# First attention group's score pieces interleaved with the last six QKV tiles

## What is computed

```python
x = x + 0.5 * ffn(layernorm(x), w1, mean_w1, w2, mean_w2, w3, mean_w3)
x = x + attn(layernorm(x), w_qkv, b_qkv, w_dense, b_dense)
x = x + 0.5 * ffn(layernorm(x), ...)
# attn:
qkv = hidden @ w_qkv.T + b_qkv           # per kv head: 4 q heads, 1 k, 1 v, of 16 columns each
q, k = rope(q, cos, sin), rope(k, cos, sin)
scores = q @ k.T * (1 / 16); scores = where(causal mask, scores, min)
ctx = softmax(scores) @ v                # 32 query heads, 8 kv heads
out = ctx @ w_dense.T + b_dense
```

## Time and profile before

| | |
|---|---|
| runs (3) | 1590.87, 1591.80, 1592.49 us; median 1591.8 |
| the profiled execution | 1592.39 us, of which the trace's span is 1590.7 us |
| PE busy | 1474.8 us, 93% of the span |
| DVE busy | 873.8 us, 55% |
| ACT busy | 643.4 us, 40% |
| QKV tiles 0 to 15 | 530 to 617 us from the span's start |
| stage 0, stage 1 | 626 to 654 us, 654 to 682 us |
| stages 2 to 15 | 682 to 1040 us |

### The profile page before, as it was taken

One profiled execution on the slowest core, in us unless ns is written; L12 is line 12 of the kernel. 1 busy time (PEld: TensorE's weight loads), 2 busy tenths in 40 slices (PEclk: granted clock), 3 DMA queues, 4 the chain that ended last, 5 costly groups with the idle time before them and its releaser, 6 DMA issues.

```text
span 1590.7 us, 25041 instructions
## 1 busy us (share of the span) xinstructions
PE 1474.8 (93%) x9584; PEld 659.8 (41%) x9584; DVE 873.8 (55%) x1375; ACT 643.4 (40%) x903; POOL 149.9 (9%) x217
## 2 busy tenths in 40 slices
PE   0788999899999987799999999989999999999998
PEld 0233444344444443334343444324444444444443
DVE  7979432432544476899999999923431422412212
ACT  4464111121122254388888888781211112112111
POOL 0320000000000143012121212210000000000000
PEclk9989999999999998599999999999999999999999
DMA  9501800000000001000000000024000000000000
GB/s 389 195 0 53 354 0 0 1 0 0 1 0 1 1 1 34 1 2 2 2 2 3 2 3 2 2 102 177 0 0 0 28 0 0 27 0 1 27 0 27
DMA packets 16459, 57.38 MB, mean 36 GB/s; under 512 B 4848, under 2 KB 4848, under 8 KB 15856
## 3 DMA queue, kind: packets, MB, share of 16 engines
q1 hardware_dynamic: 16368, 56.11, 9.1%
HBM read 40.63 MB, written 15.20 MB: 35 GB/s over the span
## 4 chain that ended last, share of the span: by engine, by line
PE 83%; DVE 9%; ACT 3%; issue 3%; DMA 0%; POOL 0%; DVEq 0%; ACTq 0%; POOLq 0%
PE ps L1232 32%; PE ps L1253 16%; PE ps L1491 9%; PE ps L1406 7%; PE ps L1472 5%; PE ps L1393 3%; PE ps L1589 3%; PE ps L1279 2%; PE ps L1226 1%; DVE rowmax L1120 1%; PE ps L1501 1%; DVE wbase L877 1%; ACT probs L706 1%; PE ps L1365 1%; DVE w_raw L842 1%
## 5 line engine op out<-in xcount | busy, mean ns | idle before, releaser
L1232 PE MATMUL ps<-xt_hi,w_all 128*128 128x512 f16 x896 | 283.3, 388 | 42.3 <-DVE w_all L883 19.7
L706 ACT ACTIVATE probs<-ps 128x1024 f32<-128x1024 f32 (+3 forms) x384 | 294.1, 814 | 48.5 <-PE ps L1472 45.5
L1120 DVE TENSOR_REDUCE rowmax<-ps 128x2 f32<-128x1024 f32 (+3 forms) x208 | 237.1, 1140 | 15.7 <-PE ps L1414 7.4
L971 DVE SCALAR_TENSOR_TENSOR hb<-ps,scal,silub 128x512 f32<-128x512 f32 x56 | 42.0, 751 | 266.6 <-PE ps L1232 266.6
L1406 PE MATMUL ps<-ka,qa 48*128 48x512 f16 (+3 forms) x768 | 165.7, 345 | 15.4 <-DVE rowmax L1120 9.2
L1232 PE MATMUL ps<-xt_lo,w_all 128*128 128x512 f16 x448 | 173.9, 388 | 0.0
L1491 PE MATMUL ps<-probs,vs 128*32 128x512 f32 (+3 forms) x1536 | 164.4, 500 | 1.4 <-ACT ctx_sb L725 0.8
L1232 PEld LDWEIGHTS ps<-xt_hi,w_all 128*128 128x128 f16 (+1 forms) x896 | 89.4, 100 | 155.9 <-issue 46.0
L1124 DVE TENSOR_REDUCE rowmax<-ps 128x1 f32<-128x512 f32 x192 | 131.2, 684 | 16.3 <-PE ps L1406 13.5
L1472 PE MATMUL ps<-qa,ka 50*128 50x512 f16 (+3 forms) x768 | 133.3, 330 | 3.7 <-ACT probs L706 3.0
L1253 PE MATMUL ps<-w32b_all,hhib 128*128 (+1 forms) x448 | 133.3, 379 | 0.0
(11 more groups left out here) (154 smaller groups left out, 2160.8 us busy)
## 6 DMA issues: line engine op xcount, KB each, us to landing
spill<-w_all SPq DMA_DIRECT2D x1, 10752.0 KB, 28.8
w32b_all<-spill SPq DMA_DIRECT2D x1, 7168.0 KB, 20.9
x<-x_in SPq DMA_DIRECT2D x4, 1024.0 KB, 5.3
y_out<-x SPq DMA_DIRECT2D x4, 1024.0 KB, 4.2
wbase<-m1t SPq DMA_DIRECT2D x4, 896.0 KB, 12.7
w_raw<-w1t SPq DMA_DIRECT2D x4, 896.0 KB, 14.2
wbase<-m3t SPq DMA_DIRECT2D x4, 896.0 KB, 24.3
w_raw<-w3t SPq DMA_DIRECT2D x4, 896.0 KB, 24.3
```

The source lines that it names most:

```text
L706: nc.scalar.activation(probs[u % PBUF][:, 2 * pair:2 * pair + 2, 0:q1 - q0], wide(("scores", g, (u, pair)))[:, :, 0:q1 - q0], ACT.Exp, sca ...
L971: nc.vector.scalar_tensor_tensor(out=bufs["h"][u][:, :], in0=ps[:, UP, :], scalar=scal[:, 1:2], in1=bufs["silu"][u][:, :], op0=ALU.mult, o ...
L1120: nc.vector.tensor_reduce(dst, src, AX.X, ALU.max).then_inc(pair_taken, 1)
L1232: last = mm(ps[:, bank, :], w[a][:, k, bass.ts(t, P)], xt[b][:, k, :], start=(k == 0 and n == 0), stop=(k == HB - 1 and n == 2))
```

## The change

The three transposes and copies of group 0 now stand after tile 9 (`EARLY = 10` tiles come first). From tile 10 on, each tile's two halves on PE are followed by two of group 0's pieces each, four to a tile; piece 24 comes after tile 15. DVE's reductions are set between the steps of the tile chain in the same way. The transposes of group 1, which stood among the pieces of stage 0, come after tiles 13, 14 and 15. The banks of tiles 10 to 15 are no longer chosen by the parity of i but are turns in `WIDE`, and their `take_raw` counts up `wide_taken` instead of `raw_ready`. Stage 0 of the pipeline loop is gone, and the loop runs from k = 1. What is computed is the same.

```diff
+EARLY = 10
+FIRST_TURNS = [("qk", 0, 0), ("qk", 0, 1), ("qk", 0, 2), ("qkv", 0, 10), ("qkv", 0, 11), ("qkv", 0, 12), ("qkv", 0, 13),
+               ("qk", 1, 0), ("qkv", 0, 14), ("qk", 1, 1), ("qkv", 0, 15), ("qk", 1, 2)]
...
-WIDE = turns(WIDE_TURNS, [("qk", 0, o) for o in range(3)])
+WIDE = turns(WIDE_TURNS, FIRST_TURNS)
...
+    def raw_taken(eng, i):
+
+        if i < EARLY:
+            eng.wait_ge(raw_ready, i + 1)
+        else:
+            eng.wait_ge(wide_taken, drained(("qkv", 0, i)))
...
@@ ACT
-        for i in range(TOKEN_TILES):
+        for i in range(EARLY):
...
-        high_parts(TOKEN_TILES - 1)
         for o in range(3):
             take_qk(0, o)
+        for i in range(EARLY, TOKEN_TILES):
+            take_raw(i)
+            take_v(i)
+            high_parts(i - 1)
+            if i >= TOKEN_TILES - 3:
+                take_qk(1, i - TOKEN_TILES + 3)
+        high_parts(TOKEN_TILES - 1)
...
@@ DVE
-        for k in range(GROUPS + 2):
+        for i in range(EARLY, TOKEN_TILES):
+            r = 4 * (i - EARLY)
+            reduce_piece(0, r)
+            add_turned(i - 1)
+            reduce_piece(0, r + 1)
+            low_parts(i - 1)
+            reduce_piece(0, r + 2)
+            along(i)
+            reduce_piece(0, r + 3)
+        add_turned(TOKEN_TILES - 1)
+        reduce_piece(0, NP_ - 1)
+        split_rowmax(0)
+        low_parts(TOKEN_TILES - 1)
+        for k in range(1, GROUPS + 2):
...
@@ PE
-        pe.wait_ge(raw_ready, TOKEN_TILES)
+        pe.wait_ge(raw_ready, EARLY)
         for o in range(3):
             transpose_qk(0, o)
-        for k in range(GROUPS + 2):
+        for i in range(EARLY, TOKEN_TILES):
+            r = 4 * (i - EARLY)
+            qkv(i, 0)
+            score_piece(0, r)
+            score_piece(0, r + 1)
+            qkv(i, 1)
+            score_piece(0, r + 2)
+            score_piece(0, r + 3)
+            if i >= TOKEN_TILES - 3:
+                transpose_qk(1, i - TOKEN_TILES + 3)
+        score_piece(0, NP_ - 1)
+        for k in range(1, GROUPS + 2):
```

More of the change, by code:

```diff
@@ L103 @@
 ]
+EARLY = 10
+FIRST_TURNS = [("qk", 0, 0), ("qk", 0, 1), ("qk", 0, 2), ("qkv", 0, 10), ("qkv", 0, 11), ("qkv", 0, 12), ("qkv", 0, 13),
+               ("qk", 1, 0), ("qkv", 0, 14), ("qk", 1, 1), ("qkv", 0, 15), ("qk", 1, 2)]
 def turns(period, first):
     out = list(first)
-    for k in range(GROUPS + 2):
-        out += [(what, k - lag, n) for what, lag, n in period if 0 <= k - lag < GROUPS and (what, k - lag) != ("qk", 0)]
+    for k in range(1 if first else 0, GROUPS + 2):
+        out += [(what, k - lag, n) for what, lag, n in period if 0 <= k - lag < GROUPS]
     return {use: n for n, use in enumerate(out)}
 TURN = turns(SINGLE_TURNS, [])
-WIDE = turns(WIDE_TURNS, [("qk", 0, o) for o in range(3)])
+WIDE = turns(WIDE_TURNS, FIRST_TURNS)
 def unit_cols(u):
@@ L677, in take_raw, with take_v @@
                 act.wait_ge(turned_ready, 2 * (i - 1))
-            b0 = 2 * (i % 2)
-            nc.scalar.activation(qkv_raw[i % 2][:, :].rearrange("p (s n) -> p s n", s=2), ps[:, b0:b0 + 2, 0:QKV // 2],
-                                 ACT.Copy, scale=scal[:, 3:4]).then_inc(raw_ready, 1)
+            nc.scalar.activation(qkv_raw[i % 2][:, :].rearrange("p (s n) -> p s n", s=2), qkv_banks(i)[:, :, 0:QKV // 2],
+                                 ACT.Copy, scale=scal[:, 3:4]).then_inc(raw_ready if i < EARLY else wide_taken, 1)
+        def take_v(i):
+            raw_taken(act, i)
+            nc.scalar.copy(v_all[:, i, :, :].rearrange("p h d -> p (h d)"), qkv_raw[i % 2][:, ROT:QKV])\
+                .then_inc(v_ready, 1)
         act.wait_ge(spilled, 16)
-        for i in range(TOKEN_TILES):
+        for i in range(EARLY):
             if i in (6, 7):
@@ L687, in _ @@
             take_raw(i)
-            act.wait_ge(raw_ready, i + 1)
-            nc.scalar.copy(v_all[:, i, :, :].rearrange("p h d -> p (h d)"), qkv_raw[i % 2][:, ROT:QKV])\
-                .then_inc(v_ready, 1)
+            take_v(i)
             if i:
                 high_parts(i - 1)
-        high_parts(TOKEN_TILES - 1)
         for o in range(3):
             take_qk(0, o)
+        for i in range(EARLY, TOKEN_TILES):
+            take_raw(i)
+            take_v(i)
+            high_parts(i - 1)
+            if i >= TOKEN_TILES - 3:
+                take_qk(1, i - TOKEN_TILES + 3)
+        high_parts(TOKEN_TILES - 1)
         def exps(g, u, pair):
@@ L1062, in along @@
         def along(i):
-            dve.wait_ge(raw_ready, i + 1)
+            raw_taken(dve, i)
             if i >= 2:
@@ L1084, in low_parts @@
                                     in1=parts_k[:, i, :, 0:HEAD], op=ALU.subtract).then_inc(qklo_ready, 1)
-        for i in range(TOKEN_TILES + 1):
+        for i in range(EARLY):
             if i in (6, 7):
@@ L1370, in transpose_qk, with qkv @@
             last.then_inc(qkt_full, 1)
-        def qkv(i):
+        def qkv(i, s):
             m, j = divmod(i, TPC)
             xt = xt_of(4 + m)
-            if i == 0:
+            if i == 0 and s == 0:
                 pe.wait_ge(silu_ready, CHUNKS * IT)
@@ L1380, in qkv @@
                 pe.wait_ge(brow_ready, 3)
-            if i == 1:
+            if i == 1 and s == 0:
                 pe.wait_ge(resid_ready, TOKEN_TILES)
-            if i >= 2:
+            if s == 0 and i >= EARLY:
+                wide_free(("qkv", 0, i))
+            elif s == 0 and i >= 2:
                 pe.wait_ge(raw_ready, i - 1)
@@ L1387, in qkv @@
                 pe.wait_ge(xlo_ready, TPC * (5 + m))
[L1388 to L1398, removed]
+            mm(qkv_banks(i)[:, s, 0:QKV // 2], row_ones[:, :], brow[:, s * QKV // 2:(s + 1) * QKV // 2],
+               start=True, stop=False)
+            for k in range(HB):
+                for n, (a, b) in enumerate(PASSES):
+                    last = mm(qkv_banks(i)[:, s, 0:QKV // 2], xt[a][:, k, j * P:(j + 1) * P],
+                              wq[b][:, k, s * QKV // 2:(s + 1) * QKV // 2], start=False,
+                              stop=(k == HB - 1 and n == 2))
+            if s == 1:
+                last.then_inc(qkv_full, 1)
+        for i in range(EARLY):
             if i in (6, 7):
```

11 lines of the change are left out of this document (5 added, 6 removed).

## The result

Medians of seven runs of each kernel: before 1591.09 us (1590.47 to 1592.59), after 1598.11 us (1597.23 to 1599.72), ratio 1.0043 [1.0033, 1.0053]: **0.4% slower**, against a forecast of 1600 with a range of 1594 to 1608. The profiled run of after took 1599.72 us, with a span of 1598.0 against 1590.7.

The account below looks back on a forecast made before the run. It took a ring of waits through PE, ACT and DVE to bound the merged tiles: 2.4 us later at full clock plus 5.6 us of low clock, 8.0 on 1592.4, less 0.6, so 1600 us, range 1594 to 1608.

Parts of the forecast that it names:

- the ring: Tiles 10 to 15: reductions, L, H, T and PE's halves wait in a loop; five tiles take 48.3 us, against 23.2.
- The rival without a ring: Merged stretch bound by DVE's work alone, 41.4 us, first reduction of stage 1 at 637.4: 1574.7 us, 8%.
- The ring at full clock: Tile 10 to stage 1, no low clock: first reduction at 657.05, 2.4 us later; as a rival 1594.2 us, 12%.
- L done 3.96: Each merged tile: DVE is free for the next step 3.96 us after T(i) starts, taken from the earlier trace.
- The clock, 5.6 us: PE falling to 1.2 GHz between tiles 11 and 13 adds 2.5 for tile 12, 2.05 for 13, half that for 11.
- The entry rival: Ahead of tile 10: group 0's transposes do not keep the clock up, another 2 us, +10 in all; no separate chance.
- Stage 1, no change: Stage 1 starts with PE idle, clock at 1.2 GHz as before, and takes the same 26.76 us: no gain.
- the bound of "up to 1 us": Dense weights' load moves into stage 1 ahead of four small DMAs: priced at 0, up to 1 us.
- the wait before piece 7: Tile 11 to 12: PE idle about 4.5 us before piece 7, counted as sure to lower the clock.
- the sum of tile 12 to 13: T(12) to T(13): chain through R(10), C, R(11), R(12), piece 13 and a half takes 10.1 us.
- the last rival's time: Stage 1 at full clock beside a short ring: +2.4 + 2 - 2.5, 1593.5 us, 4%.

Follow-up runs that it names:

- either joint: After with H(i-1) ahead of T(i) on ACT, or instead with L(i-1) behind R(r+3) on DVE: 1579.46 us each.
- those repaired kernels: After with the wait loop opened on ACT (H(i-1) ahead of T(i)) or on DVE (L(i-1) behind R(r+3)): 1579.46 us each.
- with PE kept busy: After, order unchanged, with 87 extra matmuls of unused result where PE would wait: 1588.05 us, 0.9980 of before.
- with H first: After with H(i-1) ahead of T(i) in ACT's queue in tiles 10 to 15: 1579.46 us, 0.9925 of before.
- With L last: After with L(i-1) moved behind R(r+3) on DVE, ACT's order unchanged: 1579.46 us, 0.9927 of before.
- the fourteen matmuls that held the clock: After with extra matmuls at the entry only, six before group 0's transposes and eight inside them: 1597.14 us, 1.0037 of before.
- taking it out of tile 12's way: After with piece 7 moved on PE behind the first half of tile 12: 1596.04 us, 1.0031 of before.
- holding the clock up: Before with 152 extra matmuls on PE in the seam's hole, stage 0 and the first fifteen pieces of stage 1: 1589.13 us, 0.9983 of before.
- the fillers that lifted its clock to 0.88: After with H first, L last, piece 7 moved and 51 extra matmuls at piece 24 and in stage 1: 1582.69 us, 0.9944 of before.

## Why the prediction was right

The direction, the time (1598.1 for 1600) and the mechanism were right; two terms of the sum were wrong by some 4.5 us each and cancelled.

- **What bounds the ring**: shown. The rows of after are those that were named (T rows 9.8 to 12.1 us apart; DVE idle ahead of each `parts_q` row and released by ACT's `parts_k`, for 2.4 to 5.0 us where 2 to 3 had been written), and opening either joint gave 18.6 us. The rival without a ring (1574.7) turned out to be near the arithmetic of those repaired kernels: 637.4 for the first reduction of stage 1, 640.60 and 641.34 measured.
- **The ring at full clock, "the first reduction of stage 1 2.4 us later"**: this step failed, by size and by sign. Counted from T(9), it came 65.70 us after it in before, was forecast at 68.16, and with PE kept busy came at 63.6 (62.28 and, as in after, 1.35 for the split and L(15)): 2.1 us *earlier*. The term at fault is "L done 3.96". It was taken from the earlier trace rows, where L runs beside POOL's products and takes 1.32 us, and POOL's pair 2.31. In the ring POOL is all but done when L starts (612.57 and 612.44): its pair takes 1.67 and L 0.69, and DVE is free 3.33 us after T (609.92 to 613.25). That is 0.63 us in each of six tiles, 3.8 of the 4.5 us. The trace of before had a cheaper row, L(15) with POOL idle:

```profile
623.03 0.69 DVE L1081 TENSOR_TENSOR parts_q<-rot,parts_q 128x512 f16<-128x512 f32 x1 [1.42 <-ACT parts_k L669]
```

  ACT is not what lengthens L: with H first, L(10) takes 0.69 us (605.94) beside ACT's T(11) (605.98). With L last it takes 1.31 us where it falls within POOL's pair (L at 622.61, the pair from 621.05 to 623.38) and 0.68 where it stands behind it (636.47). The Trainium skill, SBUF — State Buffer, "SBUF: two separate sides", says that a DVE operation with two SBUF inputs and a GpSimd operation that reads SBUF lock each other out of one pair of ports; the traces agree in that both are longer when they overlap (1.32 for 0.69, and 2.31 for 1.67).
- **The clock, 5.6 us**: wrong by 4.4. It was 8.9 in the five periods, where two and a half falls had been counted, and 1.1 at the entry. The falls came in all tiles: the prediction priced a fall by the length of single idle times, and called tiles 14 and 15 unlikely with 1.25 + 1.3 us of it. They paid 1.7 and 1.4.
- **The entry rival**: the clock did fall there, and its price was 1.1 us, not 2. The Trainium skill, TensorE: Matmul & The Clock Gate, Part 4, says that transposes do not count as PE activity the way products do. The trace fits that, since it fell after sixteen of them, but does not show it: the 2.3 us of idle time around them would do as well, and the fourteen matmuls that held the clock filled both.
- **Stage 1, no change**: it grew by 1.8 us. 0.8 of it is L(15), which now stands behind the split and which the sum had counted (1.55 with the split, measured 1.35); so the stage itself is about 1 us longer, within the bound of "up to 1 us" that was given for the load in it. Which of the load, the low clock (0.66 for 0.69) and the transposes took it was not tried. The forecast stopped at the first reduction of stage 1; this 1.0 us and the 1.4 us behind stage 15 have opposite signs, and the median of before came out 0.7 us lower than the 1591.8 it started from.
- **The rest**: the wait before piece 7 was 3.79 us, not 4.5, for the same 0.63 us; taking it out of tile 12's way gave 2.1 us in the median. That the fall of the clock behind stage 15 would be absent, 1.4 us in after's favour, could not have been read from before. Three slips in the working change nothing: R(10) and R(11) have each other's time in the sum of tile 12 to 13, the rival's work adds up to 41.3 and not 41.4, and the last rival's time is 1593.7.

With only the clock term right the forecast would have been 1604.4, with only the ring term right 1595.5. That both were wrong by as much, with opposite signs, is luck; the range, made from the bounds of the terms, holds either.

## What to carry to other kernels

When two loops are merged, follow one buffer round all in-order queues before counting work: if a step waits on one engine behind a step that waits for the next iteration, the loop's period is the sum of a latency chain and not the load of any engine, and exchanging two lines on one of the engines (18.6 us here) was worth more than its longest wait (2.1) or its low clock (10.0). Take the durations of such a chain from rows with the same neighbours on the other engines. And where PE works in short bursts between waits, price the low clock in every iteration, because in a latency chain its matmuls count almost in full (1.6 us lost in a period with 3.5 us at 1.2 GHz), while beside an engine that is busier than PE (stage 0 of before, all of it at 0.50) holding the clock up gave less than 1 us.

## What the runs showed of the hardware

- The clock fell behind short idle times too: 0.65 and 1.21 us with one matmul between them were followed by about 3.5 us at 1.2 GHz ((1 - 0.83) x 2 x 10.34). The stretch 135 to 145 us in the earlier trace rows, 6.58 us busy at 1.00, had not let this be seen.
- After such a fall PE worked on without a break (busy for 4.00 of 4.00 us from 629 to 633 at a mean of 0.58, ten matmuls of a half at 1.2 GHz among it), the clock rose again, and it fell again behind the next waits: one low time per tile, 3.1 to 3.5 us each, and 6.8 in tile 12 ((1 - 0.72) x 2 x 12.10) behind the 3.79 us.
- Low time that was prevented at one place came back elsewhere in the one profile that shows it (the entry: 1.13 us gained, 1.09 lost).
- DVE's L took 1.32 us beside POOL's products and 0.69 without them, also beside ACT's T; POOL's two products 2.31 and 1.67.
- What stays open: how to tell transposes from idle time as the cause of the fall at the entry; why stage 1 takes 28.1 to 28.5 us in all the repaired kernels and not the 25.5 of the later stages, (the fillers that lifted its clock to 0.88 filled PE as well); and what makes the fall of the clock behind stage 15 appear in before and two of the others, and not in the rest.
